# Which DMA queue carries what at the start of a graph network's four layers

## The chip, the cores and the metric

The kernel runs on one core of a Trainium2 chip. The metric is the device time of one launch in microseconds, the median of several runs. Before the change it is 147.41 us (three runs, 146.43 to 148.14).

## What is computed

Four graph layers on 2048 nodes with 64 features, all over the same 2048 x 2048 matrix `adj` of zeros and ones. Each layer adds its result to its input and normalises each row:

```
x = layernorm(x + L0(x, adj))   # relu([x, (adj@x + x)/deg] @ W + b), rows to unit length
x = layernorm(x + L1(x, adj))   # tanh([x, t] @ W1 + b1) @ W2 + b2 + adj@(x B') - deg * x B'
x = layernorm(x + L2(x, adj))   # w @ (x @ weight) + bias; w halves with each later neighbour, 100 at most
x = layernorm(x + L3(x, adj))   # tanh map of x, adj @ that, artanh map, @ kernel + bias
```

The weights of layer 2 depend on a running count of neighbours along each row of `adj`.

## The kernel before

The matrix is read once, in float32 (16.8 MB), and kept in SBUF as bfloat16, transposed. It comes in 16 row tiles of 1 MB, `m` = 0 to 15. A tile is four DMAs of 256 KB, one for each quarter of the columns, and each quarter goes to 32 partitions: SP's queue loads the quarters 0 and 1 (`load_lower`, L270), ScalarE's queue the quarters 2 and 3 (`load_upper`, L428). Both halves of a tile count up one semaphore, and VectorE transposes the tile (`transposes`, L661: two instructions, L667 and L668) when all four quarters are there. There are eight places for tiles that have just landed (`slot_of`, L243): tiles 0 to 7 need no wait, a later one waits for the transposes of the tile whose place it takes.

X (512 KB) is four DMAs, by partitions of 32; its rows are 64 floats, so it moves in pieces of 256 bytes. Constants (`cb`) and the packed weights are each two DMAs, of the lower and of the upper 64 partitions. The weights come in two parts: layer 0's own (up to column `first`) early, the others behind tile 11 (`WEIGHTS_BEHIND`).

Every engine's order of work is written out by hand, and an engine does nothing out of its order. VectorE begins so: maximum of |X| (L831, waits for all of X); transposes of tile 0; four small operations that make a power-of-two scale from the maximum, after GpSimd has reduced it over the partitions (L380); transposes of tile 1; the low part of X (L844), after ScalarE's high part (`split_high`, L435); transposes of tiles 2 to 5; degrees; tiles 6 and 7; then the first chunk of layer 0 between the later tiles. TensorE begins with 24 warm-up matmuls on a tile of zeros (`keep_busy`, L1132) once the maximum is there, then counts on tiles 0 and 1, 4 more warm-up matmuls, and then the transposes of X (L986), which need L844. ScalarE issues its DMAs up to tile 6, then runs its first activation; the upper halves of the later tiles are issued between its activations.

Of the kernel before, what the change touches and what calls it, by code (L numbers as in the profile page):

```python
# [15 lines left out]
U16 = mybir.dt.uint16  # L16
# [3 lines left out]
QD = 32  # L20
NQ = P // QD
# [21 lines left out]
def column_ranges(widths):  # L43
    at, out = 0, {}
    for name, w in widths.items():
        out[name] = (at, at + w)
        at += w
    return out, at


def gnn_kernel(nc, x, adj, wpack, cpack, out):
    N, D = x.shape
    NB = N // P
# [5 lines left out]
    WR, WTOT = column_ranges(WCOLS)  # L59
# [4 lines left out]
    with ExitStack() as ctx:  # L64
        def sb(name, shape, dt):
            return ctx.enter_context(nc.sbuf_tensor(name, shape, dt))
# [4 lines left out]
        def sem(name):  # L71
            return ctx.enter_context(nc.semaphore(name))
# [5 lines left out]
        X = sb("X", [P, NB, D], F32)  # L78
        Z = sb("Z", [P, NB, D + 1], F32)
        XB = sb("XB", [P, NB, D], F32)  # L80
        weights = sb("weights", [P, WTOT], F32)
        cb = sb("cb", [P, CTOT], BF16)
# [42 lines left out]
        x_loaded = sem("x_loaded")  # L125
        consts_loaded = sem("consts_loaded")
        own_weights_loaded = sem("own_weights_loaded")
        weights_loaded = sem("weights_loaded")
# [71 lines left out]
        def layer_chunk(l, e):  # L200
            return NE * l + e
# [41 lines left out]
        def slot_of(m):  # L243
            return m if m < 8 else m - 8 if m < 12 else m - 6 if m < 14 else m - 14
# [4 lines left out]
        def slot(s):  # L249
            if s < SLOTS:  # L250
                return stage[:, s]
            flat = WT[:, s // 2].rearrange("p k n -> p (k n)").bitcast(F32)
            return flat[:, (s % 2) * N:(s % 2 + 1) * N].rearrange("p (Q j) -> p Q j", Q=NQ)

        xd = x.rearrange("(q c b) f -> q b c f", q=NQ, b=QD)
# [3 lines left out]
        def store(queue, h, q):  # L259
            cs = chunk(2 * h, 2)  # L260
            queue.dma_start(od[q][:, cs], X[QD * q:QD * (q + 1), cs]).then_inc(stored, 16)

        lower, upper = slice(0, P // 2), slice(P // 2, P)
        first = WR["W1"][0]
# [3 lines left out]
        @block.sync  # L268
        def _(sp):
            def load_lower(m):  # L270
                if m >= ALL_SLOTS:
                    sp.wait_ge(transposed, m - 8 + 1 if m < 12 else m - 6 + 1)
                for q in range(NQ // 2):
                    sp.dma_start(slot(slot_of(m))[QD * q:QD * (q + 1)], ad[m, q]
                                 ).then_inc(filled[slot_of(m)], 16)

            for q in range(NQ // 2):
                sp.dma_start(X[QD * q:QD * (q + 1)], xd[q]).then_inc(x_loaded, 16)
            load_lower(0)
            load_lower(1)  # L280
            sp.dma_start(cb[lower].bitcast(U16), cpack[lower]).then_inc(consts_loaded, 16)
            sp.dma_start(weights[lower, 0:first], wpack[lower, 0:first]).then_inc(own_weights_loaded, 16)
            for m in range(2, NB):
                load_lower(m)
                if m == WEIGHTS_BEHIND:
                    sp.dma_start(weights[lower, first:WTOT], wpack[lower, first:WTOT]).then_inc(weights_loaded, 16)
            sp.wait_ge(x_ready, layer_chunk(3, 1) + 1)
            for q in range(NQ):
                store(sp, 0, q)
            sp.wait_ge(x_ready, layer_chunk(3, 3) + 1)  # L290
            for q in range(NQ // 2):
                store(sp, 1, q)
            sp.wait_ge(stored, 16 * 2 * NQ)
# [133 lines left out]
        def _(act):  # L427
            def load_upper(m):  # L428
                if m >= ALL_SLOTS:
                    act.wait_ge(transposed, m - 8 + 1 if m < 12 else m - 6 + 1)  # L430
                for q in range(NQ // 2, NQ):
                    act.dma_start(slot(slot_of(m))[QD * q:QD * (q + 1)], ad[m, q]
                                  ).then_inc(filled[slot_of(m)], 16)
# [49 lines left out]
            def take_step(i):  # L483
                for h in range(PAIRS):
                    take_chain(i, h)
# [52 lines left out]
                act.wait_ge(power_ready, 1)  # L538
                nc.scalar.activation(xs[:, 5:6], power[:, 1, 0:1], ACT.Ln)

            for q in range(NQ // 2, NQ):
                act.dma_start(X[QD * q:QD * (q + 1)], xd[q]).then_inc(x_loaded, 16)
            load_upper(0)
            load_upper(1)
            act.dma_start(cb[upper].bitcast(U16), cpack[upper]).then_inc(consts_loaded, 16)
            act.dma_start(weights[upper, 0:first], wpack[upper, 0:first]).then_inc(own_weights_loaded, 16)
            for m in range(2, 7):
                load_upper(m)
            split_high()
            take_xt(0, 0)  # L550
# [13 lines left out]
            load_upper(10)  # L564
            take_step(0)
            load_upper(11)
            act.dma_start(weights[upper, first:WTOT], wpack[upper, first:WTOT]).then_inc(weights_loaded, 16)
            take_step(1)
            take_step(2)
            load_upper(12)  # L570
# [368 lines left out]
        def _(pe):  # L939
# [192 lines left out]
            def keep_busy(n):  # L1132
                for _ in range(n):
                    nc.tensor.matmul(psC[:, 0], later[:, 0, 0:P], later[:, 0], start=True, stop=True)  # L1134

            pe.wait_ge(later_zero, 1)
            pe.wait_ge(xmax_ready, 1)
            keep_busy(24)
            pe.wait_ge(consts_loaded, 32)
            pe.wait_ge(transposed, 2)  # L1140
            counts(0, front)
# [178 lines left out]
```

## Time and profile before

| | us |
|---|---|
| median of 3 runs (range) | 147.41 (146.43 to 148.14) |
| the profiled execution, its own time | 146.32 |
| its span, first to last instruction | 144.4 |
| PE busy, of the span | 114.5 (79%) |
| DVE busy | 92.2 (64%) |
| ACT busy | 69.7 (48%) |
| POOL busy | 62.1 (43%) |
| granted TensorE clock, mean | 0.971 of full |

The profile is one execution on the one core. Busy shares are averages over stages that have different limits: in the first third the DMA engines are busy all the time, in the rest hardly at all. q1 in the rows is the queue that SP issues on, q10 that of ScalarE (SPq and ACTq where an issuing instruction is meant). A share of a queue in a window is the time that its packets took, over 16 engines times the window; a packet there is one contiguous piece, 256 bytes of X or 2 KB of the matrix, and each DMA also has one piece of 4 bytes for each engine that counts up the semaphore.

### The profile page before, as it was taken

The page shows a single profiled execution, that of the slowest core. Times are in us where ns is not written, and L with a number is a line of the kernel's source. Part 1 is how long each engine was busy: PE and PEld are TensorE (multiplying, and loading weights), DVE is VectorE, ACT ScalarE, POOL GpSimd, SP SyncE. Part 2 cuts the span into 40 slices and gives each one's busy share as a digit, 9 for nine tenths or more (in the row PEclk, how much of TensorE's full clock was granted, in tenths as well). Part 3 has the DMA queues.
Part 4 walks back from the last instruction along what each step waited for, and adds up shares of the span by engine and source line. Part 5 has one row for each costly group of instructions (what it writes and reads, how often), then busy time and mean ns, then how long its engine had stood idle before and what let it go on. Part 6 is the DMA issues. An engine that isn't in the chain of part 4 may idle for free.

```text
span 144.4 us, 3366 instructions
## 1 busy us (share of the span) xinstructions
PE 114.5 (79%) x1360; PEld 69.0 (48%) x1372; DVE 92.2 (64%) x215; ACT 69.7 (48%) x112; POOL 62.1 (43%) x90
## 2 busy tenths in 40 slices
PE   0089998987969869969798999999899899996000
PEld 0033477844725364745244756874465544565000
DVE  0229888879899997967750242555006888658970
ACT  0003355595785946869889371240334314337220
POOL 2010001094848889954329242244005353852670
PEclk9999999999999999999999999999999999999855
DMA  5999999999999993000000000000000000000006
GB/s 125 200 342 338 353 351 352 352 348 351 352 351 351 357 355 138 5 0 0 5 0 0 5 0 0 5 0 0 5 0 0 0 0 0 2 5 0 0 18 127
DMA packets 14000, 18.74 MB, mean 130 GB/s; under 512 B 5409, under 2 KB 5537, under 8 KB 13985
## 3 DMA queue, kind: packets, MB, share of 16 engines
q1 hardware_dynamic: 7536, 9.40, 21.3%
q10 hardware_dynamic: 6448, 9.13, 19.4%
q8 instruction: 11, 0.18, 0.5%
q14 instruction: 5, 0.03, 0.1%
HBM read 18.00 MB, written 0.52 MB: 128 GB/s over the span
## 4 chain that ended last, share of the span: by engine, by line
PE 40%; DVE 17%; DMA 16%; ACT 16%; issue 5%; POOL 2%; ACTq 1%; POOLq 1%; another core or an unknown queue 0%; DVEq 0%
DMA WT<-adj 10%; ACT WT L480 10%; PE psN L959 8%; PE psC L959 8%; DMA stage<-adj 6%; PE psS L959 5%; DVE AT L668 4%; PE psS L1020 3%; DVE AT L667 3%; POOL root L353 2%; PE psH L1116 2%; PE psH L1117 2%; DVE t L826 2%; ACT stage L454 2%; PE psH L1012 1%
## 5 line engine op out<-in xcount | busy, mean ns | idle before, releaser
L480 ACT ACTIVATE WT<-psC 128x1024 int16<-128x1024 f32 x32 | 30.7, 1026 | 6.3 <-PE psC L1062 5.8
L353 POOL TENSOR_TENSOR root<-var,power 128x4 f32<-128x4 f32 (+1 forms) x14 | 16.7, 1198 | 28.4 <-DVE var L741 13.6
L1020 PE MATMUL psS<-AT,XP 128*128 128x256 bf16 (+1 forms) x144 | 16.7, 261 | 0.5 <-ACT cnt L458 0.4
L667 DVE STREAM_TRANSPOSE AT<-stage 128x1024 bf16<-128x1024 bf16 x10 | 13.2, 1316 | 3.7 <-DMA stage<-adj 3.7
L1134 PE MATMUL psC<-later 128*128 128x512 bf16 x28 | 9.0, 492 | 7.7 <-DVE xs L831 7.7
L1020 PEld LDWEIGHTS psS<-AT,XP 128*128 128x128 f16 x144 | 12.0, 98 | 3.8 <-issue 2.3
L959 PE MATMUL psN<-AT,XP 128*128 128x512 bf16 x46 | 11.6, 379 | 2.1 <-ACT cnt L458 1.3
L668 DVE STREAM_TRANSPOSE AT<-stage 128x1024 bf16<-128x1024 bf16 x10 | 12.7, 1274 | 0.0
L761 DVE TENSOR_TENSOR t<-psH,XB 128x256 f32<-128x256 f32 x4 | 1.7, 424 | 16.5 <-PE psH L1117 8.9
L959 PE MATMUL psS<-AT,XP 128*128 128x512 bf16 x46 | 11.4, 379 | 0.2 <-issue 0.2
L1057 PE MATMUL psC<-later,cb 32*32 32x512 bf16 x256 | 9.3, 385 | 2.3 <-ACT WT L480 2.3
L501 ACT ACTIVATE v<-t 128x256 f32<-128x256 f32 x12 | 5.0, 416 | 11.5 <-DVE t L761 8.9
L366 POOL TENSOR_TENSOR XB<-X,weights 128x256 f32<-128x256 f32 x12 | 8.3, 710 | 4.9 <-DVE X L750 4.9
L750 DVE TENSOR_TENSOR X<-t,root 128x256 f32<-128x256 f32 x14 | 6.5, 484 | 5.3 <-POOL root L353 5.3
L1134 PEld LDWEIGHTS psC<-later 128*128 128x128 bf16 x28 | 3.2, 119 | 12.8 <-issue 11.5
L667 DVE STREAM_TRANSPOSE AT<-WT 128x1024 bf16<-128x1024 bf16 x6 | 8.0, 1331 | 1.9 <-DMA WT<-adj 1.9
L1062 PE MATMUL psC<-AT,cb 32*32 32x512 bf16 x256 | 9.1, 374 | 0.0
L959 PE MATMUL psC<-AT,XP 128*128 128x512 bf16 x31 | 7.7, 379 | 0.1
L668 DVE STREAM_TRANSPOSE AT<-WT 128x1024 bf16<-128x1024 bf16 x6 | 7.7, 1281 | 0.0
L437 ACT ACT_TABLE_LOAD x1 | 1.3, 1283 | 13.3 <-issue 13.3
L959 PE MATMUL psC<-WT,XP 128*128 128x512 bf16 x32 | 7.6, 379 | 0.0
L330 POOL TENSOR_TENSOR Z<-Z,weights 128x256 f32<-128x256 f32 x4 | 2.8, 690 | 10.8 <-ACT Z L441 10.8
(173 smaller groups left out, 235.1 us busy)
## 6 DMA issues: line engine op xcount, KB each, us to landing
stage<-adj SPq DMA_DIRECT2D x20, 256.0 KB, 12.2
stage<-adj ACTq DMA_DIRECT2D x20, 256.0 KB, 12.2
WT<-adj SPq DMA_DIRECT2D x12, 256.0 KB, 14.3
WT<-adj ACTq DMA_DIRECT2D x12, 256.0 KB, 14.9
out<-X SPq DMA_DIRECT2D x6, 64.0 KB, 1.8
X<-x SPq DMA_DIRECT2D x2, 128.0 KB, 2.9
X<-x ACTq DMA_DIRECT2D x2, 128.0 KB, 4.1
weights<-weights_packed SPq DMA_DIRECT2D x1, 160.8 KB, 16.0
```

Source lines behind the costliest of these rows:

```text
L353: nc.gpsimd.tensor_tensor(root[:, e, 0:n], var[:, e, 0:n], power[:, 0:n, 0:NR], ALU.pow).then_inc(root_ready, 1)
L366: nc.gpsimd.tensor_tensor(XB[:, chunk(e)], X[:, chunk(e)], per_feature(W(f"b{l}")), ALU.add).then_inc(xb_ready, 1)
L480: nc.scalar.activation(WT[:, e, tiles], psC[:, PAIRS * h:PAIRS * (h + 1)], ACT.Relu).then_inc(chain_taken, 1)
L501: nc.scalar.activation(v[:, chunk(e), 0:D], t[:, chunk(e)], ACT.Square, scale=0.125).then_inc(square_ready, 1)
L667: nc.vector.transpose(to[:, :, :, :, 0], halves[:, :, 0, :, :, 1])
L668: nc.vector.transpose(to[:, :, :, :, 1], halves[:, :, 1, :, :, 1]).then_inc(transposed, 1)
L750: nc.vector.tensor_tensor(X[:, chunk(e)], t[:, chunk(e)], per_node(root[:, e, 0]), ALU.mult).then_inc(x_ready, 1)
L959: ins = nc.tensor.matmul(sum_bank(l, e), XP[:, l % 2, c], matrix, start=(c == 0), stop=last)
L1020: nc.tensor.matmul(psS[:, cols], XP[:, 0, c], AT[:, c, e, cols], start=(c == 0), stop=False)
L1057: nc.tensor.matmul(psC[QD * g:QD * (g + 1), q], C("base")[rows, QD * c:QD * (c + 1)], later[rows, e % 2], start=True, stop=False)
L1062: ins = nc.tensor.matmul(psC[QD * g:QD * (g + 1), q], C("own")[rows], AT[rows, NQ * m + g, e], start=False, stop=True)
L1134: nc.tensor.matmul(psC[:, 0], later[:, 0, 0:P], later[:, 0], start=True, stop=True)
```

## The change

ScalarE's queue now carries all four DMAs of X, and behind them only its quarters of the matrix. SP's queue begins with its quarters of tile 0, then takes both halves of the constants, both halves of layer 0's weights, its quarters of tile 1, and so on; it also takes both halves of the other weights, behind tile 11. The first warm-up on TensorE is 20 matmuls instead of 24.

```diff
-            for q in range(NQ // 2):
-                sp.dma_start(X[QD * q:QD * (q + 1)], xd[q]).then_inc(x_loaded, 16)
             load_lower(0)
-            load_lower(1)
-            sp.dma_start(cb[lower].bitcast(U16), cpack[lower]).then_inc(consts_loaded, 16)
-            sp.dma_start(weights[lower, 0:first], wpack[lower, 0:first]).then_inc(own_weights_loaded, 16)
-            for m in range(2, NB):
+            for half in (lower, upper):
+                sp.dma_start(cb[half].bitcast(U16), cpack[half]).then_inc(consts_loaded, 16)
+            for half in (lower, upper):
+                sp.dma_start(weights[half, 0:first], wpack[half, 0:first]).then_inc(own_weights_loaded, 16)
+            for m in range(1, NB):
                 load_lower(m)
                 if m == WEIGHTS_BEHIND:
-                    sp.dma_start(weights[lower, first:WTOT], wpack[lower, first:WTOT]).then_inc(weights_loaded, 16)
+                    for half in (lower, upper):
+                        sp.dma_start(weights[half, first:WTOT], wpack[half, first:WTOT]).then_inc(weights_loaded, 16)
...
-            for q in range(NQ // 2, NQ):
+            for q in range(NQ):
                 act.dma_start(X[QD * q:QD * (q + 1)], xd[q]).then_inc(x_loaded, 16)
-            load_upper(0)
-            load_upper(1)
-            act.dma_start(cb[upper].bitcast(U16), cpack[upper]).then_inc(consts_loaded, 16)
-            act.dma_start(weights[upper, 0:first], wpack[upper, 0:first]).then_inc(own_weights_loaded, 16)
-            for m in range(2, 7):
+            for m in range(7):
                 load_upper(m)
...
             load_upper(11)
-            act.dma_start(weights[upper, first:WTOT], wpack[upper, first:WTOT]).then_inc(weights_loaded, 16)
             take_step(1)
...
-            keep_busy(24)
+            keep_busy(20)
             pe.wait_ge(consts_loaded, 32)
```

The order of SP's instructions from the start of the program, before and now (`stage` and `WT` are the places for landed tiles, `cb` the constants; a row is a run of equal DMAs with the shape of one):

```order
 L268 UNCONDITIONAL_BRANCH
-L278 DMA X<-x 32x16x64 x2
-L274 DMA stage<-adj 32x4x512 x4
-L281 DMA cb<-constants_packed 64x1057
-L282 DMA weights<-weights_packed 64x193
-L274 DMA stage<-adj 32x4x512 x4
+L274 DMA stage<-adj 32x4x512 x2
+L279 DMA cb<-constants_packed 64x1057 x2
+L281 DMA weights<-weights_packed 64x193 x2
+L274 DMA stage<-adj 32x4x512 x6
 L274 DMA WT<-adj 32x4x512 x8
```

X is gone from SP's queue; one tile's lower quarters stand first, and four DMAs of constants and weights come before tile 1.

The same for ScalarE, up to its first activation:

```order
 L426 UNCONDITIONAL_BRANCH
-L542 DMA X<-x 32x16x64 x2
-L432 DMA stage<-adj 32x4x512 x4
-L545 DMA cb<-constants_packed 64x1057
-L546 DMA weights<-weights_packed 64x193
-L432 DMA stage<-adj 32x4x512 x4
+L542 DMA X<-x 32x16x64 x4
+L432 DMA stage<-adj 32x4x512 x8
 L432 DMA WT<-adj 32x4x512 x6
 L437 ACT_TABLE_LOAD
```

Tile 0's upper quarters now stand behind four DMAs of X instead of two; the constants and weights are gone from between the tiles.

## Rows read from the trace of the kernel before

**Rows 1.** The page, 40 slices of the span: DMA share in tenths, GB/s.

```profile
DMA  5999999999999993000000000000000000000006
GB/s 125 200 342 338 353 351 352 352 348 351 352 351 351 357 355 138 5 0 0 5 0 0 5 0 0 5 0 0 5 0 0 0 0 0 2 5 0 0 18 127
```

**Rows 2.** VectorE in order of time: start, duration, instruction, idle time before and its releaser.

```profile
6.36 1.22 DVE L831 TENSOR_REDUCE xs<-X 128x1 f32<-128x1024 f32 x1 [6.36 <-DMA X<-x]
10.34 1.32 DVE L667 STREAM_TRANSPOSE AT<-stage 128x1024 bf16<-128x1024 bf16 x1 [2.77 <-DMA stage<-adj]
...
13.38 1.32 DVE L667 STREAM_TRANSPOSE AT<-stage 128x1024 bf16<-128x1024 bf16 x1
...
15.78 1.24 DVE L844 SCALAR_TENSOR_TENSOR XP<-X,xs,XP 128x1024 f16<-128x1024 f32 x1
17.50 1.32 DVE L667 STREAM_TRANSPOSE AT<-stage 128x1024 bf16<-128x1024 bf16 x1 [0.48 <-DMA stage<-adj]
...
32.76 1.34 DVE L667 STREAM_TRANSPOSE AT<-WT 128x1024 bf16<-128x1024 bf16 x1 [0.47 <-DMA WT<-adj]
34.00 1.27 DVE L668 STREAM_TRANSPOSE AT<-WT 128x1024 bf16<-128x1024 bf16 x1
...
37.66 1.32 DVE L667 STREAM_TRANSPOSE AT<-stage 128x1024 bf16<-128x1024 bf16 x1
```

**Rows 3.** SP's DMA issues in order of time: start, duration of all of the row.

```profile
0.72 0.90 SPq L278 DMA_DIRECT2D X<-x  x2
1.68 1.90 SPq L274 DMA_DIRECT2D stage<-adj  x4
3.62 0.93 SPq L281 DMA_DIRECT2D cb<-constants_packed  x1
4.60 0.70 SPq L282 DMA_DIRECT2D weights<-weights_packed  x1
```

**Rows 4.** Line 542, X on ScalarE's queue (two DMAs): time from issue to landing.

```profile
DMA to landing us min/median/max: 3.1/4.1/5.2
```

**Rows 5.** DMA in 1:2 (40 slices), 2:3, 3:4, 4:7 us: GB/s; packets, MB, share.

```profile
GB/s 0 0 0 0 0 0 0 0 0 0 0 0 0 0 0 0 0 0 0 0 0 0 0 0 0 0 0 0 0 20 92 92 133 174 184 256 184 205 195 143
...
q1 hardware_dynamic: 480, 0.12, 52.1%
...
DMA packets 944, 0.25 MB, mean 250 GB/s; under 512 B 935, under 2 KB 935, under 8 KB 944
...
q1 hardware_dynamic: 421, 0.12, 82.9%
...
DMA packets 361, 0.57 MB, mean 191 GB/s; under 512 B 89, under 2 KB 89, under 8 KB 361
...
q1 hardware_dynamic: 169, 0.32, 64.3%
```

**Rows 6.** The same for 17:25 us (three rows) and 5:8 us (two rows).

```profile
DMA packets 1544, 2.82 MB, mean 352 GB/s; under 512 B 169, under 2 KB 169, under 8 KB 1544
...
q1 hardware_dynamic: 771, 1.41, 53.2%
q10 hardware_dynamic: 773, 1.41, 52.8%
...
q1 hardware_dynamic: 214, 0.39, 57.6%
q10 hardware_dynamic: 212, 0.39, 35.6%
```

**Rows 7.** TensorE in order of time: first transposes of X, two waits for VectorE.

```profile
17.45 0.39 PE L986 MATMUL psX<-cb,XP 128*128 128x128 bf16 x4
...
35.33 0.62 PE L1012 MATMUL psH<-AT,cb 128*32 128x256 bf16 x16 [0.73 <-DVE AT L668]
...
42.58 0.62 PE L1012 MATMUL psH<-AT,cb 128*32 128x256 bf16 x16 [1.13 <-DVE AT L668]
```

**Rows 8.** GpSimd's reduction of the maximum over the partitions.

```profile
10.33 0.38 POOL L380 PARTITION_ALL_REDUCE xs<-xs  x1 [8.96 <-issue]
```

## The prediction

> **What bounds the kernel now.** I read the page's slices first. The DMA row stands at 9 from the third slice on and falls off in the sixteenth, at about 340 to 357 GB/s, and nothing big moves after that [rows 1]: the first 55 of 144.4 us are the load of the matrix. Then VectorE's instructions in order of time, since each tile of the matrix passes through its two transposes. Before the transposes of tiles 2 to 7 VectorE is idle some 0.5 us, each time ended by a DMA (the first and the last of the six are shown); those of tile 7 start at 32.76 and end at 35.27. From tile 8 on no DMA wait is shown [rows 2]. So the start is set by landings, and whatever moves the end of tile 7's transposes moves all that follows, one for one, unless TensorE has slack there. Its two waits for transposes in that stretch are 0.73 and 1.13 us [rows 7]. Third, the DMA queues in small windows. Two things are to be seen. In every window in which both queues have work they move equal **numbers** of packets, 771 against 773 in 8 us; in 5:8 they move 214 against 212 although SP's took 57.6% of the engines' time and ScalarE's 35.6% [rows 6]. The engines take turns by packet, not by bytes and not by time. And the packets differ: one of X (256 B) takes 0.521 x 16 / 480 = 17.4 ns [rows 5], one of the matrix (2 KB) 0.532 x 128 / 687 = 99 ns, where 687 is 1.41 MB in packets of 2 KB [rows 6].
>
> **The change, part by part.** Bytes are the same, and so is the number of DMAs. What changes is which packets stand opposite each other. Before, X is on both queues, so a packet of X has a packet of X opposite it, and X lands by 6.4 us: the last piece on ScalarE's queue takes 5.2 us from its issue, beside 3.1 for the first [rows 2, 4]. Now the 2048 packets of X, 128 for each of the 16 DMA engines, are all on ScalarE's queue, and SP's queue holds packets of 2 KB from its first instruction.
>
> First term, X. The first packets of the kernel come at 1.7, 1.0 us after the first issue (the slices of 1:2 are 25 ns each, [rows 5]). SP's issue costs are 1.90 us for four matrix DMAs, 0.93 for constants and 0.70 for weights [rows 3]. Its second tile is therefore issued at 0.72 + 0.95 + 2 x 0.93 + 2 x 0.70 = 4.9, and moves from 5.9. Until then 4.2 us pass. For each engine SP's queue has in this time 16 matrix packets (1.6 us), 8 of constants (0.8, by their bytes) and 8 of weights (0.3). To that comes what the first matrix packets cost above their 99 ns. In 3:4 SP's 421 packets took 13.3 us; 9 of all packets are matrix (944 less 935) and the other 412 of SP's need 7.2, so 5.2 us is above normal. In 4:7 they took 30.9 us for 0.32 MB, which normally needs 15.4 [rows 5]. Together 20.6 us, 1.3 for each engine, on SP's packets only. Both shares of the full windows sum to 106%, since neighbours overlap a little [rows 6], so SP's 4.0 us fill 3.8. That leaves 0.4 us, some 24 packets of X. The other 104 each wait for one matrix packet, as SP can go on with the lower halves of tiles 1 to 7 (7 x 16 = 112 packets) without waiting for anything: 104 x (99 + 17.4) / 1.06 ns = 11.4 us. **X lands at about 17.3** instead of 6.4. The bounds: with no extra cost of the first packets 28 packets of X are left at 5.9 and X lands at 9.0; with half of it 65 are left and it lands at 13.0; with a slow last engine (5.2 against 3.1 us, [rows 4]) at 19.4. Below all of these stands rival 2. I take the full cost, because the rows show it on the queue that reads the matrix first, and that is again SP's.
>
> Second term, VectorE. Its first instruction is the maximum of X (1.22 us), and everything of VectorE stands behind it in order. Tile 0's upper quarters follow X on ScalarE's queue: 16 packets beside the last 8 of SP's, 2.2 us, to 19.5. By the distances of [rows 2]: transposes of tile 0 at 19.5; those of tile 1 3.04 later at 22.5; the split (L844) 2.40 later, at 24.9 to 26.1; then six tiles of 2.50 and 0.3 for the degrees, to 41.4. All lower halves are long there, and ScalarE's queue, alone on the engines from 18 on, needs 1.5 us for an upper half, less than the 2.50 that VectorE takes. The end of tile 7 is 41.4 instead of 35.27: **+6.1 us**. Between the maximum of X and the scale lies GpSimd's reduction, over 3.1 us after the maximum by its row [rows 8]; by VectorE's rows it and the four small operations behind it are done at the latest 5.8 after the maximum, at 13.38. With 3.1 it is hidden by tile 0's transposes; with 5.8 it adds 18.5 + 5.8 - 22.5 = 1.8.
>
> Third term, TensorE. Its first real matmuls on X follow L844, now 9.1 us later than 17.0. The waits of 0.73 and 1.13 us [rows 7] swallow 1.9 of it, so that TensorE is 7.2 late where VectorE is 6.1 late. I take **+6.7** for the two, and nothing behind it gives this back: from 37.66 on VectorE is late as a whole and the later tiles have landed before it needs them.
>
> Fourth, the rest. ScalarE issues three DMAs less (constants, own weights, later weights) and two of X more; its first activation waits for the scale, which is now later than its issues, and the later weights' DMA stood between activations that wait for TensorE, so this is worth 0. The later weights, twice 160.8 KB, are now on SP's queue behind tile 11, 0.9 us of engine time that was split before; by then SP leads by whole tiles, so 0. The four warm-up matmuls that go (24 to 20) are worth 0: they run before the wait for tile 1, and from the maximum's end (18.5) to tile 1's (25.0) there are 6.5 us, less than the 8.3 between 7.6 and 15.9 that 24 of them filled.
>
> Sum: against the profiled execution's own time 146.3 + 6.7 = 153.0 us. It is 1.1 under the median of the runs, and 147.4 + 6.7 = 154.1. I forecast the median.
>
> The Trainium skill, "DMA: Bandwidth & Descriptors", section "Queues, rings and completion order", says that an engine drains a packet of typically 9 to 17 descriptors of one ring before it switches. What the profile calls a packet would then be one descriptor. By that rule the sum would be the first rival's instead of mine.
>
> **The rivals.** (1) A turn holds many packets, **148.7 us**. If an engine moves ten or more packets of X in one turn, X is done in a dozen turns: it needs its own 2.2 us beside SP's 4.0, and lands near 8. Then only a lead of SP's queue remains: while tile 0's upper half moves, tile 1's lower half does too, so each tile is complete one half tile (0.52 MB at 352 GB/s = 1.5 us) later, less at most 0.9 us that the engines gain with work from both queues in 4:7, where only 191 GB/s flow now [rows 5]. Tile 7 lands 0.6 to 1.5 us late. For it: equal packet counts would also come from long turns on both sides. Against it: after 4.0 only 89 packets under 512 B moved on all engines up to 7 [rows 5], five or six for each, and still the last of X landed at 6.4; with long turns one turn would have taken them. The section of the skill named above is this rival's rule; the row just given speaks for turns of one.
> (2) SP's first tile costs X nothing, **146.2 us**, faster. The slow first matrix packets (1.3 us for each engine) now lie beside X, which needs only the gaps, and both queues feed the engines from 1.7 on. DMA work that now starts at full rate only at 6 to 7 us [rows 1] starts about a microsecond sooner, tile 7 with it. It decides if X has landed by about 7 and tile 0 by 9.5. Against it: SP alone has 4.0 of the 4.2 us filled.
> (3) Half the cost: the extra of the first matrix packets is only half as large beside X's small ones. X lands at 13.0; 128 turns of two matrix packets, 23.9 us, bring tile 7's upper half to 36.9, and the end of its transposes to 39.4, **+4.1, 151.5 us**. The mechanism is mine, and I count it with my forecast.
> (4) The order of issue on the two queues does not matter, since the engines are shared, 147.4 us. The same page of the Trainium skill, in "Issuing engines are not separate DMA queues", says that issuing on several engines saves only issue time. The equal counts are against it: they make it matter who stands opposite whom.
>
> **How the numbers follow.** My mechanism 65%, rival 3 in it with 20 (own range 151 to 157: from half the extra cost to a slow last engine and the late scale), rival 1 18%, rivals 2 and 4 12% together, 5% for something slower still. Rival 1 lies on both sides of the bound of 1% (148.9), which is about what a measurement of this kernel tells from no change. So faster by over 1% 0.07, within 1% 0.20, slower by over 1% 0.73. For the range I leave out the faster rivals and the very slow rest: 147.8 to 157.
>
> **What would show it.** Right: DVE L831 starts at 17 to 18 instead of 6.36; in 6:16 the queues move equal counts, all of ScalarE's 256 B; tile 0's transposes start near 20, and those of tiles 2 to 7 follow with no DMA wait. Wrong: L831 before 10, with the waits of 0.47 us before tiles 2 to 7 still there (rivals 1, 2), or an X that is early and a tile 0 that is late.

## The result, and the profile after

The changed kernel takes **151.37 us** (median of 4 runs, 150.72 to 152.27) and the kernel before beside it 147.17 (4 runs, 146.43 to 148.14). The ratio is 1.0275, 95% interval 1.0225 to 1.0324: slower by 4.2 us. Some executions of a kernel are a few per cent longer at a lower granted clock than its others; every ratio here and below is of the other, fast ones of both kernels and so is not the quotient of the medians given, which are of all executions. The forecast was 154.1 in a range of 147.8 to 157. The profiled execution took 151.41 us, 5.1 more than that of before (146.32), with a span of 149.5.

VectorE in order of time (start, duration, instruction, idle time before with its releaser), as in [rows 2]; its lines stand five lower, so L826 was L831, L839 was L844 and L662 was L667:

```profile
11.06 1.22 DVE L826 TENSOR_REDUCE xs<-X 128x1 f32<-128x1024 f32 x1 [11.06 <-DMA X<-x]
14.05 1.32 DVE L662 STREAM_TRANSPOSE AT<-stage 128x1024 bf16<-128x1024 bf16 x1 [1.77 <-DMA stage<-adj]
...
17.09 1.32 DVE L662 STREAM_TRANSPOSE AT<-stage 128x1024 bf16<-128x1024 bf16 x1
...
19.48 1.24 DVE L839 SCALAR_TENSOR_TENSOR XP<-X,xs,XP 128x1024 f16<-128x1024 f32 x1
20.63 1.31 DVE L662 STREAM_TRANSPOSE AT<-stage 128x1024 bf16<-128x1024 bf16 x1
...
26.26 1.34 DVE L662 STREAM_TRANSPOSE AT<-WT 128x1024 bf16<-128x1024 bf16 x1 [0.54 <-DMA WT<-adj]
...
33.66 1.36 DVE L662 STREAM_TRANSPOSE AT<-WT 128x1024 bf16<-128x1024 bf16 x1 [1.55 <-DMA WT<-adj]
...
36.63 1.33 DVE L662 STREAM_TRANSPOSE AT<-WT 128x1024 bf16<-128x1024 bf16 x1 [0.42 <-DMA WT<-adj]
37.86 1.27 DVE L663 STREAM_TRANSPOSE AT<-WT 128x1024 bf16<-128x1024 bf16 x1
...
41.52 1.32 DVE L662 STREAM_TRANSPOSE AT<-stage 128x1024 bf16<-128x1024 bf16 x1
```

X lands at 11.06 instead of 6.36. Tile 7 starts at 36.63 instead of 32.76 and its transposes end at 39.13 instead of 35.27: **+3.9 us**, and tile 8 is still 3.9 late (41.52 against 37.66). Between the two, VectorE catches up on X: tile 2 starts 3.1 late (20.63 against 17.50) and waits for no DMA. From tile 4 on (26.26) it waits for landings again, and those are late as well. So two things are late, X and the stream of the matrix, and the second sets the end. How much of it comes from the late start alone can be read off: tile 2 starts at 20.63, and six tiles of 2.50 and 0.3 for the degrees would end at 35.9 if no tile were waited for, 0.7 later than before. The other 3.2 us are waits for landings.

Each of these is one execution. In the three profiles with X on both queues and the constants split in step (the kernel before, and twice with a shorter warm-up, below) tile 7 starts at 32.76, 33.92 and 32.25, and X lands at 6.36, 5.03 and 6.74; with the changed kernel's order of DMAs, in two profiles, tile 7 starts at 36.63 and 36.93 and X lands at 11.06 and 11.29. The difference is clear of that scatter, its size is known to about a microsecond.

DMA in 5:9, 9:12 and 12:20 us, as in [rows 5, 6] (q1 is SP's queue, q10 ScalarE's; packets, MB, share of the 16 engines):

```profile
DMA packets 1626, 0.74 MB, mean 185 GB/s; under 512 B 1415, under 2 KB 1446, under 8 KB 1626
...
q1 hardware_dynamic: 259, 0.40, 64.8%
q10 hardware_dynamic: 1367, 0.34, 53.2%
...
DMA packets 607, 0.65 MB, mean 215 GB/s; under 512 B 256, under 2 KB 353, under 8 KB 607
...
DMA packets 1507, 2.75 MB, mean 344 GB/s; under 512 B 165, under 2 KB 165, under 8 KB 1507
...
q10 hardware_dynamic: 754, 1.38, 53.2%
q1 hardware_dynamic: 753, 1.37, 52.8%
```

In 5:9 the queues move 259 against 1367 packets but 0.40 against 0.34 MB. It was not packet for packet. And the engines are full (64.8 + 53.2%) yet deliver 185 GB/s. The last of three windows has the full 344 at nearly the same share. The page's slices of GB/s, as in [rows 1], show this low rate twice:

```profile
GB/s 61 211 200 320 341 347 341 345 351 353 350 354 253 345 362 291 20 4 0 4 0 0 4 0 0 0 4 0 0 0 4 0 0 0 2 4 0 0 14 126
```

Its first four slices (3.74 us each) hold 2.96 MB by 14.95 us; those of before hold 3.81 by the same time. The 0.85 MB missing are 2.4 us at 348 GB/s. Tile 7 lands when the slices of after sum to 10.46 MB, and in before 10.06: the queue that is ahead has moved 0.40 MB of later tiles by then, another 1.1 us. Together 3.5 of the 3.87 us. The 253 in the thirteenth slice (44.9 to 48.6 us) is where SP's queue carries both halves of the later weights; in before 351 and 357 stand there.

TensorE in order of time, as in [rows 7]:

```profile
39.18 0.62 PE L1007 MATMUL psH<-AT,cb 128*32 128x256 bf16 x16 [1.47 <-DVE AT L663]
...
46.45 1.04 PE L1007 MATMUL psH<-AT,cb 128*32 128x256 bf16 x16 [1.14 <-DVE AT L663]
47.42 1.89 PE L1015 MATMUL psS<-AT,XP 128*128 128x256 bf16 x8
...
54.31 0.62 PE L1007 MATMUL psH<-AT,cb 128*32 128x256 bf16 x16
```

At 39.18 and 46.45 it is 3.85 and 3.87 late, as VectorE is. The counts at 46.45 take 1.04 us for 0.62 and the sums behind them 1.89 for 1.05, and at 54.31 TensorE is 5.13 late (49.18 in before). Three stretches with the granted clock (PEclk, the third number from the right) show why: us, then each engine's busy time.

```profile
42.00:45.80 3.80, 3.01 (x75) 1.46 (x72) 3.80 (x4) 3.12 (x4) 2.76 (x4) 1.00 1.07 326
45.80:49.20 3.40, 2.75 (x24) 1.49 (x24) 3.37 (x7) 1.42 (x2) 2.07 (x4) 0.50 1.06 265
49.20:52.60 3.40, 3.05 (x75) 1.37 (x74) 3.37 (x6) 2.67 (x3) 3.02 (x7) 1.00 1.06 353
```

In 45.8 to 49.2 the clock is at 1.2 instead of 2.4 GHz, after a stretch in which TensorE was busy 3.01 of 3.8 us. It costs 1.3 us of this execution's 5.1: from 76.24 (71.11 in before) to 145.81 (140.68) VectorE stays 5.13 late. The other executions of the changed kernel had mean clocks of 0.961 to 0.976 and times of 150.72 to 152.27.

### The profile page after: what moved, and what is told of

It reads as the page before. It is cut to its first block, busy times and chain, and to the rows that moved or that the text cites. A ratio compares the mean times of both kernels' runs of the same rounds, so it can differ in the third digit from the quotient of the medians.

```text
span 149.5 us, 3358 instructions
## 1 busy us (share of the span) xinstructions
PE 113.4 (76%) x1356; PEld 68.7 (46%) x1368; DVE 92.2 (62%) x215; ACT 69.7 (47%) x112; POOL 62.1 (42%) x90
## 3 DMA queue, kind: packets, MB, share of 16 engines
q1 hardware_dynamic: 6720, 9.48, 22.1%
## 4 chain that ended last, share of the span: by engine, by line
PE 39%; DVE 17%; DMA 16%; ACT 15%; issue 4%; ACTq 3%; POOL 2%; POOLq 1%; another core or an unknown queue 0%; DVEq 0%
DMA WT<-adj 10%; ACT WT L480 9%; PE psN L954 8%; PE psC L954 7%; DMA stage<-adj 6%; PE psS L954 5%; DVE AT L663 4%; PE psS L1015 4%; DVE AT L662 3%; POOL root L353 2%; PE psH L1111 2%; PE psH L1112 2%; PE psH L1007 2%; DVE t L821 2%; ACT stage L454 2%
## 5 line engine op out<-in xcount | busy, mean ns | idle before, releaser
L1015 PE MATMUL psS<-AT,XP 128*128 128x256 bf16 (+1 forms) x144 | 17.6, 269 | 0.5 <-ACT cnt L458 0.4
L1129 PE MATMUL psC<-later 128*128 128x512 bf16 x24 | 6.8, 443 | 12.4 <-DVE xs L826 12.4
L662 DVE STREAM_TRANSPOSE AT<-stage 128x1024 bf16<-128x1024 bf16 x10 | 13.2, 1317 | 1.9 <-DMA stage<-adj 1.8
L662 DVE STREAM_TRANSPOSE AT<-WT 128x1024 bf16<-128x1024 bf16 x6 | 8.0, 1333 | 3.0 <-DMA WT<-adj 3.0
L1129 PEld LDWEIGHTS psC<-later 128*128 128x128 bf16 x24 | 2.5, 110 | 15.9 <-issue 14.3
L1007 PE MATMUL psH<-AT,cb 128*32 128x256 bf16 (+1 forms) x144 | 5.6, 279 | 4.1 <-DVE AT L663 4.1
L826 DVE TENSOR_REDUCE xs<-X 128x1 f32<-128x1024 f32 x1 | 1.2, 1220 | 11.1 <-DMA X<-x 11.1
```

Source lines behind the costliest of these rows:

```text
L662: nc.vector.transpose(to[:, :, :, :, 0], halves[:, :, 0, :, :, 1])
L1007: ins = nc.tensor.matmul(psH[QD * g:QD * (g + 1), cols], one, AT[:, NQ * g + k, e, cols], start=(k == 0), stop=(k == NR - 1))
L1015: nc.tensor.matmul(psS[:, cols], XP[:, 0, c], AT[:, c, e, cols], start=(c == 0), stop=False)
```

## The experiments

The kernels were timed in three groups, each beside the kernel before on the same chip (before's medians there: 148.75 for the first four kernels below, 148.10 for the constants first, 24 warm-up matmuls, the first measurement with 20 and the constants on SP's queue, 147.84 for the rest). Each profile is one execution. The letters in the expectations name the theories that they state.

**X split over both queues again, the rest of the change kept**

```diff
+            for q in range(NQ // 2):
+                sp.dma_start(X[QD * q:QD * (q + 1)], xd[q]).then_inc(x_loaded, 16)
             load_lower(0)
...
-            for q in range(NQ):
+            for q in range(NQ // 2, NQ):
                 act.dma_start(X[QD * q:QD * (q + 1)], xd[q]).then_inc(x_loaded, 16)
```

> The changed kernel with X split over both queues again: pieces 0 and 1 at the head of SP's queue, 2 and 3 on ScalarE's; constants and weights stay on SP's queue, behind tile 0, and the warm-up stays at 20. Theory A (X alone on one queue, opposite large packets, is all of the cost): X lands near 6.4 us again, tile 7's transposes end at 35.3 +- 0.5, and the time is 147.2 +- 0.8. Rival B (the constants and weights on SP's queue, ahead of tile 1, cost something of their own, since SP's quarters of each tile then come later than ScalarE's): X lands near 6.4, but tile 7's transposes end 0.5 to 1 us later than before, 148 us.

Measured: median 154.1 us, ratio 1.0405 (1.0251 to 1.0559), no better than the change. X is early again (6.67), but:

```profile
16.43 1.31 DVE L664 STREAM_TRANSPOSE AT<-stage 128x1024 bf16<-128x1024 bf16 x1 [3.30 <-DMA stage<-adj]
...
52.26 1.35 DVE L664 STREAM_TRANSPOSE AT<-WT 128x1024 bf16<-128x1024 bf16 x1 [1.26 <-DMA WT<-adj]
```

Tile 1, behind both halves of constants and weights on SP's queue, starts at 16.43 (13.38 in before), and tile 12, behind the later weights, has a wait that neither kernel has. The engines deliver 224 GB/s in 9:12 here, and 361 in 13:18. Tile 7's transposes end at 37.2 instead of 35.27, more than the 0.5 to 1 us of rival B (part of it is clock: VectorE waits 1.48 us for TensorE before tile 6, and the granted clock is low in 20 to 24 us). So the constants and weights have a price of their own.

A part of the 4% is clock. At tile 13 VectorE is 0.5 us ahead of the changed kernel (55.26 against 55.74), and yet this execution takes 152.68 against 151.41. Its mean granted clock is 0.941 against 0.961, in 50 to 58 us it is 0.57, and its other three executions have 0.921 to 0.931. Whether the order of the DMAs brings the low clock about is not shown.

**X alone moved, the rest as before**

```diff
-            for q in range(NQ // 2):
-                sp.dma_start(X[QD * q:QD * (q + 1)], xd[q]).then_inc(x_loaded, 16)
...
-            for q in range(NQ // 2, NQ):
+            for q in range(NQ):
                 act.dma_start(X[QD * q:QD * (q + 1)], xd[q]).then_inc(x_loaded, 16)
```

> The kernel before with one edit: all of X on ScalarE's queue. Constants and weights stay split over both queues behind tile 1, warm-up 24. Theory A: nearly the whole cost of the change, 150.5 to 152 us, X landing near 11. If large packets opposite X count one by one (the turns of the prediction), X lands later than in the changed kernel, at 12 or more, since SP now has tile 1 to move at once. Rival B: about half of the cost, 149 us.

Measured: 152.23 us, ratio 1.0289 (1.0102 to 1.0477); X at 11.12, tile 0 at 14.23, as in the changed kernel. Within its interval, moving X is by itself as dear as the whole change. With turns of one packet X should have landed at 12 or more, since SP can move tile 1 at once; it did not. The rate is 211 GB/s in 5:9 and 238 in 9:12.

How the queues really take turns can be read here. In two neighbouring windows of 1.8 us, 5.0:6.8 and 6.8:8.6:

```profile
q1 hardware_dynamic: 128, 0.23, 69.2%
q10 hardware_dynamic: 534, 0.13, 49.1%
...
q1 hardware_dynamic: 136, 0.25, 69.2%
q10 hardware_dynamic: 538, 0.13, 45.4%
```

A DMA of X has 528 packets (512 pieces and 16 that count), one of the matrix 144. So in each 1.8 us one DMA of X and about one of the matrix move, and not evenly mixed: in steps of 0.2 us from 6.8 ScalarE's queue moves 2, 9, 38, 74, 113, 127, 97, 55 and 23 packets, a burst of one DMA, and SP's has the most where it has the least. X's four DMAs have four such turns, and 3.2 + 4 x 1.8 = 10.4 is near the landing at 11.12. In the changed kernel X begins in this way too: ScalarE's queue moves 537 packets in 3.2:5.0, of them 11 in the last 0.2 us. After that its counts are too even to read a turn from (48 to 89 in each 0.2 us from 5.4 to 9.2).

**SP waits for all of X before its first DMA**

```diff
+            sp.wait_ge(x_loaded, 16 * NQ)
             load_lower(0)
```

> The changed kernel, but SP waits until X has landed before it issues its first DMA, so that nothing stands opposite X. Theory T (the turns of the prediction: X is late because its packets wait for SP's) and theory M (small and large packets side by side slow each other in the DMA engines): X moves at the rate of 2:3 us of the kernel before, some 940 packets in a microsecond, and lands at 4.5 to 5.3 us. Theory Q (one queue hands out small packets at no more than some 350 to 520 in a microsecond, whatever the other does): X lands at 6.0 to 8.0 us. The whole kernel is slow under all three, since SP's tile 0 starts only then.

Measured, a single execution: 159.57 us. DMA in 2:4 and in 5:9:

```profile
DMA packets 1792, 0.45 MB, mean 225 GB/s; under 512 B 1790, under 2 KB 1790, under 8 KB 1792
...
DMA packets 461, 0.84 MB, mean 210 GB/s; under 512 B 51, under 2 KB 51, under 8 KB 461
...
q10 hardware_dynamic: 461, 0.84, 101.9%
```

Alone, ScalarE's queue moves X at 225 GB/s and it lands at 5.42: one queue is enough for X, and what stands opposite makes it late. The matrix alone on that queue gets 210 GB/s, with the engines full. These two rates price the turns of the kernel with X alone moved, as an estimate: 0.13 MB of X at 225 and 0.26 MB of the matrix at 210 GB/s are 0.6 + 1.2 = 1.8 us, the 1.8 found there. So its low rate fits queues that move one after the other, each at the rate that it has alone.

**X in pieces of 4 KB** (the nodes stand in another order, so the result is another one)

```diff
-        xd = x.rearrange("(q c b) f -> q b c f", q=NQ, b=QD)
+        xd = x.rearrange("(q b c) f -> q b c f", q=NQ, b=QD)
```

> The changed kernel with X read as one piece of 4 KB for each partition (128 packets instead of 2048, the same bytes); the nodes are then in another order than the matrix has them, so what is computed is not the reference. All three theories say that X lands early, near 5 us, beside SP's first tile. T and M: with the small packets gone the queues run at full rate from 3 or 4 us on, tile 0 lands by 10 and tile 7's transposes end at 34.5 to 36: 146.5 to 148 us. If the loss is instead in the order of the tiles and constants on SP's queue, 150 us or more remain.

Measured: median 149.88 us, ratio 1.0138 (1.002 to 1.0255). X lands at 9.48, with 8 pieces for each engine instead of 128, and 5:9 has 224 GB/s:

```profile
9.48 1.22 DVE L826 TENSOR_REDUCE xs<-X 128x1 f32<-128x1024 f32 x1 [9.48 <-DMA X<-x]
```

The forecast's count of turns would have brought X to the end of SP's first 8 turns, and all three theories had it near 5; all three missed. One sixteenth of the pieces took away 1.6 of the 4.7 us, so the number of pieces is the smaller part. With turns of whole DMAs that is to be expected: X is still four DMAs. That this is the reason was not tried (X as one DMA would).

**Constants and layer 0's weights first on SP's queue, tile 0 behind them**

```diff
-            load_lower(0)
             for half in (lower, upper):
                 sp.dma_start(cb[half].bitcast(U16), cpack[half]).then_inc(consts_loaded, 16)
             for half in (lower, upper):
                 sp.dma_start(weights[half, 0:first], wpack[half, 0:first]).then_inc(own_weights_loaded, 16)
-            for m in range(1, NB):
+            for m in range(NB):
                 load_lower(m)
```

> The changed kernel with constants and layer 0's weights at the head of SP's queue and tile 0 behind them. Theory C (the slow first packets of the matrix hold the engines, and X's first packet comes only at 3.2 instead of 2.0 for that reason): X's packets start near 2, most of X has moved by 5, and it lands at 6 to 8. Theory M (any large packets beside X slow it): X lands at 9 to 11 again. Tile 0 lands later than in the changed kernel by about 1 us under both.

Measured, a single execution: 153.02 us at a mean clock of 0.931. VectorE's first instruction, and DMA in 6:10:

```profile
6.79 1.22 DVE L825 TENSOR_REDUCE xs<-X 128x1 f32<-128x1024 f32 x1 [6.79 <-DMA X<-x]
```

```profile
DMA packets 509, 0.94 MB, mean 235 GB/s; under 512 B 51, under 2 KB 51, under 8 KB 509
```

With another transfer than the matrix opposite its first packets, X lands at 6.79. So the slow first packets of the matrix (39 packets take 81.5% of 16 engines in 2:3 of the changed kernel, 0.33 us each) are a large part of X's lateness. In that stretch of the changed kernel no packet of X moved at all; here 637 packets of ScalarE's queue did. But the low rate stays, 235 GB/s in 6:10, nearly all after X. Here too the queues move one after the other, although both carry the matrix: SP's 101 packets against 16 in 7:8, then 30 against 113 in 8:9. A burst is one DMA again: 138 packets of SP's queue in 6.6:8.2, 137 of ScalarE's in 7.6:9.2, where a DMA has 144. Tile 7 starts at 33.80 against 32.76. Its time does not follow from tile 7: tile 12 waits 1.16 us for a DMA, as in the first experiment, and the clock is low. One execution can't weigh the two.

**24 warm-up matmuls in the changed kernel, 20 in the one before** (the diff shows the first; the second is the reverse)

```diff
-            keep_busy(20)
+            keep_busy(24)
```

> The changed kernel with a first warm-up of 24 matmuls instead of 20. Between the end of the 20 and tile 1 the changed kernel's TensorE is idle for 1.54 us; 24 fill 0.9 of it. Rival W: half-clock stretches get fewer and the time falls by 1 us or so. Theory A: no difference, within 0.5%. X lands at 11 again in its profile if that belongs to the order of the DMAs.

> The kernel before with the change's third part alone: the first warm-up has 20 matmuls instead of 24. Theory A (the queue orders are all of the cost): within 1% of the kernel before. Rival W (with the warm-up shorter, TensorE stands idle before tile 1 is there, and the granted clock falls to half for a stretch later): 1 to 3 us slower, with half-clock stretches between 15 and 60 us. Its profile also shows the load of the kernel before a second time: if the stretch of some 225 GB/s up to 12.0 us that the changed kernel and the first four experiments show belongs to the execution and not to the order of the DMAs, it can stand here too; if it belongs to their order, 8 to 12 us run at 335 to 350 GB/s as in the first profile.

> The kernel before with 20 warm-up matmuls instead of 24, a second time and in more rounds. If the first measurement (0.9944 of before, interval 0.989 to 0.9998) was a gain: a ratio of 0.991 to 0.997 whose interval stays below 1. If it was scatter: a ratio of 0.997 to 1.003.

Measured: the changed kernel with 24, 152.18 us, ratio 1.0264 (1.0193 to 1.0334) beside 1.0275 with 20. The kernel before with 20: 0.9944 (0.989 to 0.9998), and again, in 12 executions, 1.0011 (0.9968 to 1.0055). The first was scatter. The warm-up's length is worth nothing that these intervals can tell at either place.

**Constants and layer 0's weights all on SP's queue, and all on ScalarE's, X as before** (the diff shows the first; the second is its mirror)

```diff
-            sp.dma_start(cb[lower].bitcast(U16), cpack[lower]).then_inc(consts_loaded, 16)
-            sp.dma_start(weights[lower, 0:first], wpack[lower, 0:first]).then_inc(own_weights_loaded, 16)
+            for half in (lower, upper):
+                sp.dma_start(cb[half].bitcast(U16), cpack[half]).then_inc(consts_loaded, 16)
+            for half in (lower, upper):
+                sp.dma_start(weights[half, 0:first], wpack[half, 0:first]).then_inc(own_weights_loaded, 16)
...
-            act.dma_start(cb[upper].bitcast(U16), cpack[upper]).then_inc(consts_loaded, 16)
-            act.dma_start(weights[upper, 0:first], wpack[upper, 0:first]).then_inc(own_weights_loaded, 16)
```

> The kernel before with another part of the change alone: both halves of the constants and of layer 0's weights on SP's queue, at the place behind tile 1 where its own halves stand; X stays split, warm-up 24. If the queues take turns by packet, SP's quarters of tile 2 come 4 constants and 4 weight packets for each engine later, each beside a matrix packet of ScalarE's: tile 2 lands some 1 us later than 17.5, later tiles up to 0.9 us late; 147.5 to 149 us. If only the number of bytes counts: no difference.

> The kernel before, with both halves of the constants and of layer 0's weights on ScalarE's queue behind tile 1 and none on SP's: the mirror of the kernel that had them all on SP's. Theory T (a queue that carries them brings its quarters late turn for turn, whichever queue it is): tile 2's transposes start at 19.5 to 20.5 instead of 17.50, as in the mirror, with 219 to 230 GB/s while the constants move, and 150 to 152 us. Theory U (something of SP's queue alone): no slow stretch, tile 2 later by no more than 1.0 us, 147 to 149 us.

Measured: on SP's queue 152.02 us, ratio 1.0166 (1.0017 to 1.0314), above the 147.5 to 149 expected. On ScalarE's 153.08 us (4 runs, 151.35 to 156.09), all above the 145.79 to 150.26 of before beside it. DMA in 12:15 of the two, SP's first:

```profile
DMA packets 473, 0.68 MB, mean 227 GB/s; under 512 B 75, under 2 KB 183, under 8 KB 473
q10 hardware_dynamic: 236, 0.42, 65.4%
q1 hardware_dynamic: 237, 0.26, 43.0%
```

```profile
DMA packets 476, 0.73 MB, mean 243 GB/s; under 512 B 77, under 2 KB 150, under 8 KB 476
q1 hardware_dynamic: 238, 0.43, 62.4%
q10 hardware_dynamic: 238, 0.30, 45.4%
```

The same on either queue: equal counts (here packet for packet does hold), tile 2 at 20.12 and 20.58 instead of 17.50, and 227 and 243 GB/s where before had 338 to 353 [rows 1]. So the slow stretch belongs to the imbalance, not to SP.

It is not all of the price. In 26:33 of the first kernel (us, then each engine's busy time, the granted clock third from the right), and VectorE behind it:

```profile
26.00:33.00 7.00, 7.00 (x45) 5.30 (x36) 4.85 (x4) 2.62 (x5) 0.00 (x0) 0.53 1.05 354
...
33.70 0.16 DVE L679 TENSOR_SCALAR degp<-psH 128x4 f32<-128x4 f32 x1 [2.19 <-PE psH L1042]
```

After the late tiles TensorE was busy only 1.05 of 3.6 us (21.9 to 25.5); then its clock was at the lower level for 6.9 us, although it was busy throughout, and VectorE waited 2.19 us for it. In before the same work ran at the full clock, and VectorE had no such wait. On ScalarE's queue 26:33 has 0.53 as well, and the wait is 0.90. So these two kernels lose time by the clock as well as by the DMA, and how much by each no run tells apart.

**Out of step, but each queue its own half**

```diff
             load_lower(0)
-            load_lower(1)
             sp.dma_start(cb[lower].bitcast(U16), cpack[lower]).then_inc(consts_loaded, 16)
             sp.dma_start(weights[lower, 0:first], wpack[lower, 0:first]).then_inc(own_weights_loaded, 16)
+            load_lower(1)
```

> The kernel before, with SP's half of the constants and of layer 0's weights one tile earlier (behind tile 0) than ScalarE's half (behind tile 1). Each queue keeps its bytes, its partitions and its columns; only the step differs. Theory S (the DMA engines deliver 180 to 250 instead of 350 GB/s whenever the two queues are out of step): a stretch of 3 to 5 us at 220 to 250 GB/s while SP's constants move beside ScalarE's tile 1, tile 7's transposes end 1.5 to 2.5 us later than 35.3, 149 to 150.5 us. Theory K (the slow stretch needs one queue to carry both halves of something): full rate of 340 GB/s or more from 7 us on, tile 7's transposes end at 35.0 to 35.6, the time of before within 0.7%.

Measured: ratio 0.9978 (0.9904 to 1.0051). DMA in 7:10, where SP's constants move beside ScalarE's tile 1:

```profile
DMA packets 577, 0.96 MB, mean 319 GB/s; under 512 B 79, under 2 KB 131, under 8 KB 577
q10 hardware_dynamic: 296, 0.54, 58.1%
q1 hardware_dynamic: 281, 0.42, 48.0%
```

No long slow stretch: 319 GB/s, a little below the 340 of theory K (before has 337 in 7:10), and tile 7 ends at 35.8. Being out of step by 0.18 MB is not the cause. That more would be was not tried, but the kernel with the constants on SP's queue is at 348 GB/s in 17:18 when SP's queue has carried 0.37 MB more than its share. What all kernels with a long slow stretch share is that one queue carries both halves of something, or (SP waiting) is alone.

**X's upper quarters first on ScalarE's queue**

```diff
-            for q in range(NQ):
+            for q in (2, 3, 0, 1):
                 act.dma_start(X[QD * q:QD * (q + 1)], xd[q]).then_inc(x_loaded, 16)
```

> The changed kernel, with ScalarE's four DMAs of X in the order 2, 3, 0, 1, so that in the first microseconds the two queues write different halves of the partitions (SP the lower with tile 0, ScalarE the upper with X). Theory P (both queues writing the same partitions is what slows the engines to 180 to 200 GB/s): X lands by 9.5 instead of 11.06, tile 7's transposes end by 37.8, 149.5 to 150 us. Theory not P: X at 10.7 to 11.4, tile 7 at 39.1, 151 to 152 us.

Measured: 152.22 us, ratio 1.0352 (1.0283 to 1.0421).

```profile
10.07 1.22 DVE L826 TENSOR_REDUCE xs<-X 128x1 f32<-128x1024 f32 x1 [10.07 <-DMA X<-x]
```

X lands 1.0 earlier than in the changed kernel, between the two expectations, at 210 GB/s in 5:9; tile 7's transposes end at 38.3 (39.13 in the changed kernel), and the time is no better. That both queues write the same partitions isn't the cause of the low rate; whether it adds to it stays open.

## Why the prediction was right in direction and too large

The measured 151.37 lies in the range, but none of the three signs that were named for it came: X landed at 11.06 and not at 17 to 18, the counts were not equal, and tiles 4 to 7 did wait for DMA. The direction was right for a reason that is only in part the one given, and that the size came as near as it did (+4.2 us for +6.7) is luck: X's lateness was put more than twice too high, and the slower stream, which makes 3.2 of the 3.9 us, was put at nothing.

**What bounds the kernel: right.** The delay at tile 7's transposes passes to all that follows on VectorE: +3.9 there, +3.9 at tile 8. With X alone moved (1.0289, 1.0102 to 1.0477) the whole price is there within the interval. The fastest run of the changed kernel (150.72) is above the slowest of before beside it (148.14).

**First term, X at 17.3: too large, measured 11.06.** The step that failed is "the engines take turns by packet, not by bytes and not by time". The rows behind it, 771 against 773 and 214 against 212 [rows 6], are of packets of the same 2 KB on both queues: 1.41 against 1.41 MB, 0.39 against 0.39. They exclude turns by time but can't tell turns by packet from turns by bytes or from long turns, and it is the difference between these that the term was made of. With unlike packets the trace of after shows 1367 against 259 packets, 5.3 for one. Nor was it true "in every window in which both queues have work" of the kernel before. In its 4:5, where SP's first matrix packets stand beside the last of X:

```profile
q1 hardware_dynamic: 41, 0.08, 71.6%
q10 hardware_dynamic: 78, 0.04, 15.4%
```

So X was not held up 104 times by a matrix packet. What the runs show in place of this are turns of about one DMA where X stands opposite the matrix: 538 packets of X's queue against 136 in 1.8 us with X alone moved, and by the estimate above each queue moves in its turn at the 210 to 225 GB/s that it has alone. Four such turns bring X to about 11; the 104 single ones were to bring it to 17. In the changed kernel itself only the first turn can be read. The slow first packets of the matrix came on top: without them opposite X, X lands at 6.79. This part of the term was right in kind. The piece experiment fits: 8 pieces instead of 128 for each engine took off only 1.6 us.

**Second term, +6.1 on VectorE: measured +3.9.** The distances from tile 0 to tile 1 (3.04) and on to the split (2.39) held. But the six tiles of 2.50 without a DMA wait did not: with X at 11.06 the landings set tiles 4 to 7. By this term's own sum, tile 0 at 14.05 gives 35.9 for the end of tile 7, only 0.7 late. The step that failed here is that the later tiles cost no wait, since a full rate was taken for the stream throughout. The 1.5 us for an upper half on ScalarE's queue "alone on the engines" is such a rate: the queue that was alone had 210 GB/s, by which 0.52 MB need 2.5. Of the 3.87 us at the start of tile 7, 2.4 us are bytes not moved at the low rate, and 1.1 the lead of one queue. That lead is the term of rival 1, put at 0.6 to 1.5.

**Third term, +0.6 more on TensorE: no such mechanism.** Its instructions with the waits, at 39.18 and 46.45, are 3.85 and 3.87 late. The wait of 0.73 us [rows 7] became 1.47 instead of being swallowed. The 1.3 that this execution lost later are clock, and the forecast had no term for that.

**The terms put at 0.** Warm-up: right, shown by three kernels. Later weights: right here only because VectorE is late anyway. When it is less late, tile 12 waits 0.94 to 1.26 us for a DMA (the kernels with X split, in wide pieces, and with the constants first). Constants and weights on SP's queue: put inside X's term, and alone they cost 1.7% (0.2 to 3.1) behind tile 1, and 4.05% (2.5 to 5.6) behind tile 0 with the later weights, clock included. With the latter the two moves are not additive: 4.05 and 2.9% (1.0 to 4.8) apart, 2.75% (2.25 to 3.2) together. That one's delay covers the other's is an argument; no run isolates it. That the four removed DMA issues on ScalarE were worth nothing was not tried apart.

**The rivals.** Rival 3 gave 151.5 us and 39.4 for the end of tile 7; measured 151.4 and 39.1. The number is right by luck: its X was at 13.0, by turns of one packet. Rival 1 (long turns, X near 8, 148.7) had the better mechanism and the wrong price: it took X and the matrix together at the full rate, and its time falls. Rivals 2 and 4 fall too: the order matters. For the rule of the Trainium skill, "DMA: Bandwidth & Descriptors", section "Queues, rings and completion order", that an engine drains a packet of some 9 to 17 descriptors before it switches, the traces agree in kind, and in number only for the matrix. A turn of one DMA is 144 / 16 = 9 of the profile's packets for each engine where it is of the matrix and 528 / 16 = 33 where it is of X. But constants opposite the matrix move 237 against 236, where turns of a DMA would give 5 against 9 for each engine. So no one length of turn fits all the stretches. The same page's section "Issuing engines are not separate DMA queues", by which only issue time is at stake, does not hold here: moving X alone costs a ratio of 1.0289, while ScalarE's issues of X take 2.21 us for four instead of 0.98 for two in the changed kernel, and X on that queue lands at 5.42 when nothing stands opposite.

**What stays open.** Why the queues move one after the other in one stretch, DMA by DMA at 210 to 240 GB/s, and packet beside packet in another, from 12.0 us on in the changed kernel at 344. And why the constants opposite the matrix, with equal counts, are as slow (227): bursts do not explain that stretch. The low rate is not X's small pieces (wide pieces: 224 GB/s), not the warm-up, not SP's queue (mirror), not being out of step by 0.18 MB, and not the same partitions on both alone. It begins with one queue carrying both halves of something, or moving alone, in nine of the experiments and at the later weights, and can outlast that transfer; no run isolates what sets it off.

## What to carry to other kernels

Equal counts of packets over some microseconds do not say how long a turn is: turns of one packet and turns of a whole DMA give the same counts. Look at steps of 0.2 us, and for a stretch in which unlike transfers stand opposite each other. Give each of two DMA queues the same kind of transfer at the same time, each its own half: moving one small input or the constants wholly to one queue cost 1.7 to 2.9% here with the bytes unchanged (the intervals reach from 0.2 to 4.8%). And price a late input and a slower stream apart: the later of the two sets the end, and undoing one of them may gain nothing. Look at the granted clock too before a difference is put down to the DMA: a late tile leaves TensorE idle, and the clock may fall behind it.

## What was not expected of the hardware

- The same engines at the same share of busy time (106%) moved 344 GB/s in one stretch (12:20 of the changed kernel) and 235 in another (6:10 with the constants first), both with pieces of 2 KB on both queues. In the second the queues moved one after the other.
- The queue that is alone does not get the full rate: 210 GB/s for the matrix, 225 for X.
- A matrix packet among the first takes 0.33 us in the changed kernel, three times its usual 99 ns, and no packet of X on the other queue moved in 1:3 beside it; with constants in its place 637 moved in 2:3.
- The clock falls to its lower level between 18 and 66 us in the profiled executions of 11 of the 14 kernels and repeats here. In the kernel before with 20 warm-ups it does so for 3.4 us, after a stretch in which TensorE was busy 2.60 of 3.4 us (below), and in its second profile not at all in that part. In the kernels with constants or X moved alone it is low for some 7 us from 25.5 or 27.5 on, behind the late tiles:

```profile
39.70:43.10 3.40, 2.60 (x64) 1.28 (x40) 3.40 (x4) 2.87 (x4) 2.35 (x4) 0.99 1.05 339
43.10:46.50 3.40, 2.78 (x24) 1.50 (x24) 3.37 (x7) 1.28 (x2) 2.10 (x4) 0.50 1.06 344
```
